# A transformer block on one core: TensorE's pieces at other places in the batch and in the set-up, the other engines' hand-overs reordered

## The chip, the cores and the metric

The kernel runs on one core of one Trainium2 chip. The metric is the time of one launch on the device in microseconds (us). One execution was also profiled; its rows are in a section of their own further down. Engines are named as the profile does: PE (matmuls), PEld (its weight loads), DVE (vector), ACT (scalar), POOL (GpSimd) and SP, which here only issues transfers. A kernel line such as L559 is line 559 of the kernel before; all five engine programs call the same small helper functions, so a line in the profile names a helper, and its place in the program is told by its time.

## The reference

A block with attention and a feed-forward net side by side, for 16 batches of 512 tokens and 256 features:

```
xn = layernorm(x)                                  # 16 x 512 x 256
q, k, v = xn @ wq, xn @ wk, xn @ wv                # 8 heads of 128; q and k rotated (RoPE)
p = softmax(q k' / 128 with a causal mask)         # 512 x 512 for each batch and head
attn = (p @ v) @ wo
h = relu([xn, -xn] @ (+-1 weights k0) * s0) * 2    # 1024 wide
h = relu(h @ (+-1 weights k1) * s1) * 2            # 1024 wide
ffn = h @ (+-1 weights k2) * s2
out = x + attn + ffn
```

## The kernel before, in words

Float32 values are carried as pairs of float16, a high and a low part; a product of two such pairs is three matmuls (high-high, high-low, low-high). The high part is written by ACT (`qk_hi`, `v_hi`, `o_hi`, ...), the low part by DVE, which reads the same PSUM bank again and subtracts the high part (`qk_lo` L559, `v_lo` L564, `o_lo` L569, `p_lo` L584, `h0r_lo_low` L593, `h1_lo`). There are eight PSUM banks, and each PE piece takes a whole one, so a piece can start only when the piece that used its bank before has been read by both engines.

A batch is cut into these PE pieces: `qk` (q or k of one head, 6 matmuls), `v_proj` (6), `scores` (12 matmuls in three fills), `values` (18), `layer0` (4 or 8), `product` (the middle layer of the feed-forward net, which in the loop is done by seven products of half the size in place of eight, 16 matmuls a half), `layer2` (32) and `project` (48). In the set-up batch 0 still takes the middle layer whole (`layer1`, 16 matmuls). `qk(g, w)` has g = 8b + head and w = 0 for q, 1 for k; so `scores(8b+1)` belongs to the second head of batch b.

The way of a head: `qk` on PE; ACT copies the two halves crosswise (`swap`, two instructions), DVE multiplies by the cosines (`straight`), POOL by the sines (`crossed` L351), DVE adds (`rotate` L556), ACT writes the high part and DVE the low part (L559); then `scores`; then row maxima on DVE, exponentials on ACT, both halves of the probabilities, a transposing transfer that SP issues (`turn_p`), and `values`, which reads the transposed tile pt. A next batch's normalised input goes the same way through a transposing transfer (`turn_x`, tile xT).

No scheduler decides the order at run time. Each engine has a program written out line by line with its waits (`sync_program` L742, `gpsimd_program` L888, `scalar_program` L1284, `vector_program` L2189, `tensor_program` L3603). Batches 0 and 1 are written out, `for b in range(2, 15)` holds one batch with pieces of batch b+1 and b-1 woven in, and a tail ends the last. The table `ROTATION` (L726) says which bank stands behind each of the loop's eight bank names in a batch. An engine works its list strictly in order, so a piece that stands ahead of another one on DVE delays it although nothing else ties them together.

The set-up: SP issues the loads. DVE takes the statistics of batch 0, turns the three scale factors (tile s, 1.5 KB) into signs (`scale_signs` L483), normalises (`normalise_first` L498), prepares k0 (`subtract_k0` L502), and takes the largest absolute value of each of wq, wk, wv and wo (`largest` L510). PE turns these maxima (`turn_largest`), DVE makes a power of two from them (`power_of_two` L518), and PE spreads it to all partitions:

```
dve.wait_ge(s_s3, 16)
scale_signs(dve)
dve.wait_ge(s_rstd, 1)
normalise_first(dve, 0)
...
largest(dve, 0)          # wq
largest(dve, 1)          # wk
...                      # eight h0_first_lo
power_of_two(dve, 0)     # released: PE's spread_power(0), which all qk need
```

Of the kernel before, what the change touches and what calls it, by code (L numbers as in the profile page):

```python
# [34 lines left out]
def block_kernel(nc, x, wq, wk, wv, wo, k0, k1, k2, s3, cosT, sinT, out):  # L35
    ctx = ExitStack()
    with ctx:
# [702 lines left out]
        ]  # L740

        def sync_program(sp):  # L742
            load_x_first(sp)
            load_x_rest(sp)
            load_scales(sp)
            load_k(sp, 0)
            load_k(sp, 1)
# [3602 lines left out]
```

## Time and profile before

| | |
|---|---|
| time of a launch, median of 3 | 1775.95 us (1774.67 to 1776.29) |
| the profiled execution, its own time | 1776.42 us |
| its span (first to last instruction) | 1774.5 us |
| PE busy | 1721.9 us (97%) |
| DVE, ACT, POOL busy | 1532.1, 1267.3, 927.4 us |
| granted TensorE clock, mean over the span | 0.996 |

The difference between the profiled time and its span, 1.92 us, is what lies around the program. PE is the engine to watch: what it is not busy is 52.6 us of the span, and the rows further down show where these lie and what PE waited for.

### The profile page before, as it was taken

The page shows a single profiled execution, that of the slowest core. Times are in us where ns is not written, and L with a number is a line of the kernel's source. Part 1 is how long each engine was busy: PE and PEld are TensorE (multiplying, and loading weights), DVE is VectorE, ACT ScalarE, POOL GpSimd, SP SyncE. Part 2 cuts the span into 40 slices and gives each one's busy share as a digit, 9 for nine tenths or more (in the row PEclk, how much of TensorE's full clock was granted, in tenths as well). Part 3 has the DMA queues.
Part 4 walks back from the last instruction along what each step waited for, and adds up shares of the span by engine and source line. Part 5 has one row for each costly group of instructions (what it writes and reads, how often), then busy time and mean ns, then how long its engine had stood idle before and what let it go on. Part 6 is the DMA issues. An engine that isn't in the chain of part 4 may idle for free.

```text
span 1774.5 us, 34051 instructions
## 1 busy us (share of the span) xinstructions
PE 1721.9 (97%) x12720; PEld 1195.5 (67%) x12720; DVE 1532.1 (86%) x3630; ACT 1267.3 (71%) x2717; POOL 927.4 (52%) x952
## 2 busy tenths in 40 slices
PE   6899989999999999999999999999999999999999
PEld 2456757767676676767767677676766767677667
DVE  7899888897988979888897988989889798888975
ACT  6677676776867777677776767768677776777763
POOL 6555545555545645464564555555456454655632
PEclk9999999999999999999999999999999999999999
DMA  4234543344343443344344343433434344343433
GB/s 172 48 48 79 93 68 79 66 78 76 63 92 58 87 70 64 86 67 85 59 79 89 63 81 66 78 72 66 87 65 88 67 65 85 67 87 58 80 70 73
DMA packets 454839, 134.09 MB, mean 76 GB/s; under 512 B 434704, under 2 KB 453648, under 8 KB 454672
## 3 DMA queue, kind: packets, MB, share of 16 engines
q1 hardware_dynamic: 454672, 131.90, 39.4%
q8 instruction: 100, 1.64, 0.4%
q14 instruction: 67, 0.55, 0.1%
HBM read 14.94 MB, written 8.39 MB: 13 GB/s over the span
## 4 chain that ended last, share of the span: by engine, by line
PE 68%; DVE 20%; POOL 3%; DMA 3%; ACT 3%; issue 2%; SPq 1%; DVEq 0%; POOLq 0%
PE bank L238 32%; PE bank L694 17%; PE bank L678 8%; PE bank L661 8%; DVE ph L584 3%; PE bank L705 3%; DVE bank L556 3%; DVE p L574 3%; DVE qk L559 2%; DVE bank L553 2%; DMA pt<-ph 2%; DVE rt L589 1%; POOL xT L342 1%; POOL tb L351 1%; ACT p L426 1%
## 5 line engine op out<-in xcount | busy, mean ns | idle before, releaser
L354 POOL TENSOR_SCALAR ph<-p,ri 128x384 f16<-128x384 f32 (+3 forms) x512 | 313.2, 612 | 455.4 <-DVE rk L581 418.2
L351 POOL TENSOR_TENSOR tb<-tb,sin 128x512 f32<-128x512 f32 x256 | 333.0, 1301 | 242.1 <-ACT tb L410 235.2
L694 PE MATMUL bank<-hb,wa 128*128 128x256 f16 x3360 | 379.9, 273 | 0.2 <-ACT bank L442 0.2
L694 PEld LDWEIGHTS bank<-hb,wa 128*128 128x128 fp8e5 x3360 | 328.0, 98 | 41.7 <-ACT bank L442 0.5
L426 ACT ACTIVATE p<-p,nm,sc 128x512 f32<-128x512 f32 (+3 forms) x512 | 328.5, 645 | 1.6
L584 DVE SCALAR_TENSOR_TENSOR ph<-p,rk,ph 128x512 f16<-128x512 f32 (+3 forms) x512 | 310.2, 613 | 0.7 <-POOL ph L354 0.7
L574 DVE CUSTOM_DVE_ANT_0 p<-bank,mask 128x512 f32<-128x512 f32 (+3 forms) x512 | 228.9, 484 | 48.9 <-PE bank L661 46.8
L661 PE MATMUL bank<-qk 128*128 128x512 f16 (+3 forms) x1536 | 231.6, 301 | 14.7 <-DVE qk L559 13.5
L678 PE MATMUL bank<-pt,v 128*128 128x256 f16 (+1 forms) x2304 | 232.5, 255 | 12.9 <-DMA pt<-ph 11.5
L678 PEld LDWEIGHTS bank<-pt,v 128*128 128x128 f16 x2304 | 202.5, 98 | 39.9 <-DMA pt<-ph 17.5
L661 PEld LDWEIGHTS bank<-qk 128*128 128x128 f16 x1536 | 133.3, 98 | 121.3 <-DVE qk L559 21.6
L413 ACT ACTIVATE qk<-bank 128x512 f16<-128x512 f32 x256 | 151.0, 590 | 82.1 <-DVE bank L556 81.7
L559 DVE TENSOR_TENSOR qk<-bank,qk 128x512 f16<-128x512 f32 x256 | 174.3, 681 | 31.4 <-ACT qk L413 30.3
L556 DVE TENSOR_TENSOR bank<-bank,tb 128x512 f32<-128x512 f32 x256 | 177.3, 693 | 19.2 <-POOL tb L351 14.0
L238 PE MATMUL bank<-xT,wq 128*128 128x512 f16 x768 | 186.6, 379 | 1.6 <-DVE v L564 1.6
L409 ACT ACTIVATE tb<-bank 64x512 f32<-64x512 f32 x256 | 151.9, 593 | 50.9 <-PE bank L238 42.9
L238 PE MATMUL bank<-xT,wk 128*128 128x512 f16 x768 | 186.7, 379 | 1.0 <-DVE wk L533 1.0
L238 PE MATMUL bank<-wv,xT 128*128 128x512 f16 x768 | 183.7, 379 | 2.9 <-DMA xT<-rt 2.9
L553 DVE TENSOR_TENSOR bank<-bank,cos 128x512 f32<-128x512 f32 x256 | 176.7, 690 | 4.5 <-ACT tb L410 4.5
L238 PE MATMUL bank<-wo,o 128*128 128x256 f16 x1536 | 172.9, 273 | 0.0
L358 POOL TENSOR_TENSOR hb<-rt,hb 128x1024 f16<-128x1024 f32 x60 | 132.5, 2208 | 62.1 <-ACT hb L439 60.8
L238 PEld LDWEIGHTS bank<-wo,o 128*128 128x128 f16 x1536 | 150.2, 98 | 20.5
(111 smaller groups left out, 2266.3 us busy)
## 6 DMA issues: line engine op xcount, KB each, us to landing
out<-xnat SPq DMA_DIRECT2D x32, 256.0 KB, 2.4
xnat<-in_x SPq DMA_DIRECT2D x15, 512.0 KB, 3.9
pt<-ph SPq DMA_TRANSPOSE x256, 4.3
o<-in_k SPq DMA_DIRECT2D x1, 1024.0 KB, 7.4
v<-in_wq SPq DMA_DIRECT2D x1, 1024.0 KB, 9.4
v<-in_wk SPq DMA_DIRECT2D x1, 1024.0 KB, 11.1
ph<-in_wv SPq DMA_DIRECT2D x1, 1024.0 KB, 13.5
o<-in_wo SPq DMA_DIRECT2D x1, 1024.0 KB, 10.3
```

Of the source, the lines that this page charges most:

```text
L238: m = pe.matmul(ps[:, cols[0]:cols[1]], l, r, start=start and n == 0, stop=signal is not None and n == last)
L351: pool.tensor_tensor(tb, tb, SIN[:], ALU.mult).then_inc(s_crossed, 1)
L354: pool.tensor_scalar(part(g, i, HI), prob(g, i), RI[:, g % 4, i:i + 1], 4096.0, ALU.mult, ALU.mult).then_inc(s_P_hi, 1)
L426: act.activation(prob(g, i), prob(g, i), ACT.Exp, bias=NM[:, g % 4, i:i + 1], scale=SC[:, 0:1], accum_out=SM[:, g % 4, i:i + 1]).then_inc( ...
L553: dve.tensor_tensor(ps[:, :], ps[:, :], COS[:], ALU.mult).then_inc(s_straight, 1)
L556: dve.tensor_tensor(ps[:, :], ps[:, :], TB[:, (2 * g + w) % TRING, :], ALU.add).then_inc(s_rot, 1)
L559: dve.tensor_tensor(QK[:, g % 2, 2 * w + 1, :], ps[:, :], QK[:, g % 2, 2 * w, :], ALU.subtract).then_inc(s_qk_lo, 1)
L574: dve.tensor_tensor_reduce(out=prob(g, i), in0=ps[:, a:a + w], in1=MASK[:, 512 - w:512], scale=1.0, scalar=-3.0e38, op0=ALU.add, op1=ALU.m ...
L584: dve.scalar_tensor_tensor(part(g, i, LO), prob(g, i), RK[:, g % 4, i:i + 1], part(g, i, HI), ALU.mult, ALU.subtract).then_inc(s_P_lo, 1)
L661: mm = pe.matmul(ps[:, col:col + w], l, m, start=i == tiles[0] and n == 0, stop=end)
L678: mm = pe.matmul(ps[:, 128 * i0:128 * i1], l, m, start=n == 1, stop=n == 18)
L694: mm = pe.matmul(ps[:, 256 * u:256 * u + 256], WA[:, w, k, (2 * j + u) * 128:(2 * j + u) * 128 + 128], HB[:, h, s, k, :], start=first and ...
```

## The change

The helpers are the same, and so are the operations. What differs is the order of the calls in all five programs, the waits that go with it, and the banks. Batches 0 to 3 are written out now, and the loop runs over `range(4, 15)` (`range(4, 14)` on ACT and PE); `ROTATION` has 16 rows and repeats every eight batches where it repeated every six. The core of the diff, SP's loads, one row of the table, DVE's set-up and three places of PE's loop:

```diff
         def sync_program(sp):
+            load_x_rest(sp)
             load_x_first(sp)
-            load_x_rest(sp)
+            load_k(sp, 0)
+            load_w(sp, "k")
+            load_w(sp, "q")
             load_scales(sp)
-            load_k(sp, 0)
             load_k(sp, 1)
-            load_w(sp, "q")
-            load_w(sp, "k")
-            load_cos(sp)
+            load_w(sp, "v")
             load_sin(sp)
-            load_k(sp, 2)
-            load_w(sp, "v")
-            load_x(sp, 1)
             sp.wait_ge(s_k0, 4)
             load_w(sp, "o")
+            load_cos(sp)
+            load_x(sp, 1)
+            load_k(sp, 2)
+            sp.wait_ge(s_xp, 1)
+            turn_x(sp, 1)
             sp.wait_ge(s_P_lo, 4)
             sp.wait_ge(s_pad, 1)
             turn_p(sp, 0)
             sp.wait_ge(s_P_lo, 8)
             sp.wait_ge(s_W2, 1)
             turn_p(sp, 1)
-            sp.wait_ge(s_xp, 1)
-            turn_x(sp, 1)
...
         def vector_program(dve):
...
+            dve.wait_ge(s_w_in["k"], 16)
+            largest(dve, 1)
             dve.wait_ge(s_xT_hi, 1)
             xT_first_lo(dve, 0, BANK[0])
             dve.wait_ge(s_xT_hi, 2)
             xT_first_lo(dve, 1, BANK[1])
-            subtract_k0(dve, 1)
-            subtract_k0(dve, 2)
-            subtract_k0(dve, 3)
             dve.wait_ge(s_w_in["q"], 16)
             largest(dve, 0)
-            dve.wait_ge(s_w_in["k"], 16)
-            largest(dve, 1)
             dve.wait_ge(s_h0_hi, 1)
-            h0_first_lo(dve, 0, BANK[2])
+            h0_first_lo(dve, 3, BANK[2])
+            dve.wait_ge(s_w_in["v"], 16)
+            largest(dve, 2)
...
+            dve.wait_ge(s_w_in["o"], 16)
+            largest(dve, 3)
...
+            dve.wait_ge(s_x[1], 16)
+            stats(dve, 1)
             dve.wait_ge(s_am_max, 1)
             power_of_two(dve, 0)
...
         def tensor_program(pe):
...
+            for b in range(4, 14):
+                ps = [BANK[i] for i in ROTATION[b]]
...
+                qk(pe, 8 * b + 9, 1, ps[4])
+                pe.wait_ge(s_h1, 8 * b)
+                scores(pe, 8 * b + 8, 0, ps[2])
...
+                qk(pe, 8 * b + 10, 1, ps[4])
+                pe.wait_ge(s_vp, 8 * b + 11)
+                v_proj(pe, b + 1, 0, 2, ps[3])
...
+                pe.wait_ge(s_qk_lo, 16 * b + 22)
+                v_proj(pe, b + 1, 1, 3, ps[4])
```

**SP, the first loads.** These are rows of the difference on SP. The names are the tiles and the inputs; o and v and ph are also the places where weights wait until they are split.

```order
+L249 DMA xnat<-in_x 128x2x256
 L245 DMA xnat<-in_x 128x2x256
-L249 DMA xnat<-in_x 128x2x256
+L259 DMA o<-in_k 128x4x256
+L267 DMA v<-in_wk 128x2x1024
+L267 DMA v<-in_wq 128x2x1024
 L255 DMA s<-in_s 128x3
-L259 DMA o<-in_k 128x4x256
 L259 DMA o<-in_k 128x8x256
-L267 DMA v<-in_wq 128x2x1024
-L267 DMA v<-in_wk 128x2x1024
+L267 DMA ph<-in_wv 128x2x1024
```

The scales s stood third, behind the two halves of x; now k0 (0.5 MB), wk and wq (1 MB each) go ahead of them.

**DVE, from the first transposed input to the power of two.** Before (L506 writes xT's low part, L510 is `largest`, L545 the low part of h0, L518 to L524 the power of two):

```order
L506 SCALAR_TENSOR_TENSOR xT<-bank,xT 128x4x128 x2
L502 TENSOR_TENSOR w<-o 128x2x256 x3
L510 TENSOR_REDUCE p<-v 128x1 x2
L545 SCALAR_TENSOR_TENSOR hb<-bank,hb 128x512 x5
L514 TENSOR_REDUCE ar<-bank 128x1
L545 SCALAR_TENSOR_TENSOR hb<-bank,hb 128x512 x3
L518 TENSOR_SCALAR ar<-ar 128x1
L521 TENSOR_SCALAR ar<-ar 128x1
L524 TENSOR_SCALAR dg<-ident,ar 128x2
```

Now:

```order
L510 TENSOR_REDUCE p<-v 128x1
L506 SCALAR_TENSOR_TENSOR xT<-bank,xT 128x4x128 x2
L510 TENSOR_REDUCE p<-v 128x1
L545 SCALAR_TENSOR_TENSOR hb<-bank,hb 128x512
L510 TENSOR_REDUCE p<-ph 128x1
L545 SCALAR_TENSOR_TENSOR hb<-bank,hb 128x512 x4
L510 TENSOR_REDUCE p<-o 128x1
L545 SCALAR_TENSOR_TENSOR hb<-bank,hb 128x512 x3
L514 TENSOR_REDUCE ar<-bank 128x1
L456 BN_STATS bn<-xnat 128x6 x4
L461 BN_AGGR mv<-bn 128x2 x4
L464 TENSOR_SCALAR ve<-mv 128x4
```

One `largest` moved ahead of xT's low part, the two of wv and wo (p<-ph, p<-o) and the statistics of batch 1 (L456 to L464) moved ahead of the power of two, which follows these rows. The three subtractions of L502 moved ahead of the first row.

**PE in the loop, batch 6, between k of its second head and that head's scores.** Before (after the row wk of head 1; with bank numbers, as rows would read alike):

```order
L238 MATMUL bank7<-xT,wk 128x512 x6
L238 MATMUL bank3<-wv,xT 128x512 x6
L661 MATMUL bank6<-qk 128x512 x3
...
L661 MATMUL bank1<-qk 128x256 x3
L678 MATMUL bank4<-pt,v 128x256 x9
...
L238 MATMUL bank0<-xT,wq 128x512 x6
L238 MATMUL bank6<-xT,wk 128x512 x6
L661 MATMUL bank3<-qk 128x512 x3
```

Now, from the same k of head 1 to its scores and on to the v projection that follows (the wk of bank 0 behind the scores is k of head 2, and the last row, on the same bank, is `v_proj(b, 1, 3)`):

```order
L238 MATMUL bank0<-xT,wk 128x512 x6
L661 MATMUL bank7<-qk 128x512 x3
...
L705 MATMUL bank4<-w2,h1 128x256 x32
L238 MATMUL bank5<-wv,xT 128x512 x6
L238 MATMUL bank7<-xT,w0 128x512 x4
L238 MATMUL bank2<-xT,w0 128x512 x4
L678 MATMUL bank6<-pt,v 128x256 x9
...
L661 MATMUL bank1<-qk 128x512 x3
```

```order
L238 MATMUL bank0<-xT,wk 128x512 x6
L238 MATMUL bank5<-wv,xT 128x512 x6
L238 MATMUL bank6<-xT,w0 128x512 x4
L238 MATMUL bank1<-xT,w0 128x512 x4
L238 MATMUL bank3<-xT,wq 128x512 x6
L238 MATMUL bank4<-xT,w0 128x512 x4
L238 MATMUL bank5<-xT,w0 128x512 x4
L238 MATMUL bank0<-wv,xT 128x512 x6
```

Between k of head 1 and its scores there now stands a whole `layer2` (w2,h1, 32 matmuls), and no other `qk`. The last fence is the hand-over of one bank from k of head 2 to a v projection, with five pieces between them.

## Rows read from the trace of the kernel before

**Rows 1.** The page, part 1: busy us (share of the span), instructions.
```profile
PE 1721.9 (97%) x12720; PEld 1195.5 (67%) x12720; DVE 1532.1 (86%) x3630; ACT 1267.3 (71%) x2717; POOL 927.4 (52%) x952
```

**Rows 2.** Stretches: us; busy PE, PEld, DVE, ACT, POOL; PEclk, DMA, GB/s.
```profile
25.98:90.20 64.22, 52.77 (x246) 24.22 (x245) 53.97 (x107) 43.13 (x80) 36.90 (x37) 0.92 0.18 34
90.20:270.00 179.80, 170.47 (x1220) 113.37 (x1219) 160.08 (x388) 133.54 (x296) 93.41 (x100) 0.99 0.44 71
270.00:1700.00 1430.00, 1413.72 (x10616) 996.33 (x10615) 1251.35 (x2980) 1037.27 (x2233) 758.11 (x769) 1.00 0.40 74
372.09:479.61 107.52, 106.45 (x802) 75.06 (x801) 94.24 (x226) 78.34 (x169) 57.12 (x58) 1.00 0.41 75
```

**Rows 3.** Waits of PE over the span: us in total, times, longest.
```profile
PE bank L661 <- DVE qk L559: 13.5, 16, 2.9
PE bank L678 <- DMA pt<-ph: 11.5, 20, 2.2
...
PE bank L238 <- DMA xT<-rt: 2.9, 3, 1.4
```

**Rows 4.** PE in batch 6: start, us, instruction, idle before it.
```profile
674.62 3.66 PE L705 MATMUL bank<-w,h 128*128 128x256 fp8e5 x32
678.94 1.82 PE L678 MATMUL bank<-pt,v 128*128 128x256 f16 x18 [0.66 <-DMA pt<-ph]
...
683.62 1.46 PE L238 MATMUL bank<-xT,wk 128*128 128x512 f16 x6
...
692.93 1.80 PE L661 MATMUL bank<-qk 128*128 128x512 f16 x12 [0.69 <-DVE qk L559]
```

**Rows 5.** Timeline of DVE, just ahead of the wait at 692.
```profile
691.20 0.47 DVE L584 SCALAR_TENSOR_TENSOR ph<-p,rk,ph 128x256 f16<-128x256 f32 x1
691.59 0.68 DVE L564 SCALAR_TENSOR_TENSOR v<-bank,v 128x512 f16<-128x512 f32 x1
692.20 0.67 DVE L559 TENSOR_TENSOR qk<-bank,qk 128x512 f16<-128x512 f32 x1
```

**Rows 6.** The page, part 5: the multiplication on POOL inside the rotation.
```profile
L351 POOL TENSOR_TENSOR tb<-tb,sin 128x512 f32<-128x512 f32 x256 | 333.0, 1301 | 242.1 <-ACT tb L410 235.2
```

**Rows 7.** Timeline of the loads that SP issues at the start.
```profile
1.73 0.46 SPq L255 DMA_DIRECT2D s<-in_s  x1
...
3.26 0.86 SPq L267 DMA_DIRECT2D v<-in_wq  x1
```

**Rows 8.** Loads until 30 us: KB each, us to landing.
```profile
v<-in_wq SPq DMA_DIRECT2D x1, 1024.0 KB, 9.4
...
s<-in_s SPq DMA_DIRECT2D x1, 1.5 KB, 3.2
```

**Rows 9.** Timeline of DVE in the set-up.
```profile
7.54 1.38 DVE L498 TENSOR_SCALAR rt<-xnat,mv,rs 128x256 f32<-128x256 f32 x4 [0.86 <-POOL rs L326]
...
10.71 0.69 DVE L506 SCALAR_TENSOR_TENSOR xT<-bank,xT 128x512 f16<-128x512 f32 x1 [0.50 <-ACT xT L365]
11.80 0.69 DVE L506 SCALAR_TENSOR_TENSOR xT<-bank,xT 128x512 f16<-128x512 f32 x1 [0.41 <-ACT xT L365]
...
14.35 4.47 DVE L510 TENSOR_REDUCE p<-v 128x1 f32<-128x2048 f32 x2
19.10 3.08 DVE L545 SCALAR_TENSOR_TENSOR hb<-bank,hb 128x512 f16<-128x512 f32 x5 [0.29 <-ACT hb L399]
...
59.04 1.40 DVE L456 BATCH_NORM_STATS2 bn<-xnat 128x6 f32<-128x256 f32 x4
```

**Rows 10.** Timeline of PE in the set-up.
```profile
25.98 0.28 PE L238 MATMUL bank<-dg,p 128*128 128x2 f32 x2
26.12 2.75 PE L238 MATMUL bank<-hb 128*128 128x512 f16 x12
...
39.19 5.33 PE L238 MATMUL bank<-hb 128*128 128x512 f16 x12
...
58.15 3.38 PE L661 MATMUL bank<-qk 128*128 128x512 f16 x12 [2.95 <-DVE qk L559]
```

More of the change, by code:

```diff
@@ L2424, in vector_program @@
[L2424 to L2437 removed]
+            qk_lo(dve, 4, 1, BANK[1])
@@ L3916, in tensor_program @@
[L3916 to L3924 removed]
+            product(pe, 1, 6, range(8), BANK[1])
+            pe.wait_ge(s_vp, 14)
+            product(pe, 1, 5, range(8), BANK[3], first=True)
+            pe.wait_ge(s_o, 11)
@@ new lines, in tensor_program @@
+            pe.wait_ge(s_h1, 11)
+            qk(pe, 22, 1, BANK[5])
+            pe.wait_ge(s_o, 17)
+            v_proj(pe, 2, 1, 0, BANK[3])
+            pe.wait_ge(s_pt[1], 288)
+            pe.wait_ge(s_s5, 4)
+            values(pe, 17, BANK[4])
+            pe.wait_ge(s_pt[0], 320)
+            pe.wait_ge(s_qk_lo, 45)
+            values(pe, 18, BANK[2])
+            product(pe, 0, 4, range(8), BANK[1])
+            pe.wait_ge(s_vp, 22)
+            scores(pe, 21, 0, BANK[3])
+            pe.wait_ge(s_o, 18)
@@ new lines, in tensor_program @@
+            scores(pe, 21, 1, BANK[4])
+            pe.wait_ge(s_qk_lo, 46)
+            scores(pe, 21, 2, BANK[5])
+            pe.wait_ge(s_o, 19)
+            qk(pe, 23, 1, BANK[2])
+            product(pe, 1, 2, range(8), BANK[6])
+            pe.wait_ge(s_h1, 12)
+            v_proj(pe, 2, 1, 2, BANK[1])
+            product(pe, 1, 7, range(8), BANK[7])
+            pe.wait_ge(s_pt[1], 320)
+            pe.wait_ge(s_max, 85)
+            values(pe, 19, BANK[3])
+            pe.wait_ge(s_max, 88)
@@ new lines, in tensor_program @@
+            v_proj(pe, 2, 1, 1, BANK[5])
+            pe.wait_ge(s_h1, 13)
+            qk(pe, 23, 0, BANK[6])
+            pe.wait_ge(s_copy, 12)
+            product(pe, 1, 4, range(8), BANK[4])
+            pe.wait_ge(s_qk_lo, 47)
+            scores(pe, 22, 0, BANK[2])
+            pe.wait_ge(s_vp, 23)
+            scores(pe, 22, 1, BANK[1])
+            pe.wait_ge(s_o, 20)
+            scores(pe, 22, 2, BANK[3])
+            pe.wait_ge(s_pt[0], 352)
+            pe.wait_ge(s_vp, 24)
+            values(pe, 20, BANK[7])
@@ new lines, in tensor_program @@
+            pe.wait_ge(s_xT, 48)
+            v_proj(pe, 3, 0, 1, BANK[5])
+            pe.wait_ge(s_qk_lo, 48)
+            scores(pe, 23, 0, BANK[4])
+            scores(pe, 23, 1, BANK[2])
+            scores(pe, 23, 2, BANK[6])
+            pe.wait_ge(s_max, 91)
+            qk(pe, 24, 1, BANK[1])
+            pe.wait_ge(s_max, 92)
+            qk(pe, 24, 0, BANK[3])
+            pe.wait_ge(s_o, 21)
+            layer2(pe, 0, BANK[7])
+            product(pe, 1, 3, range(8), BANK[0])
+            pe.wait_ge(s_max, 93)
@@ new lines, in tensor_program @@
+            layer2(pe, 0, BANK[6])
+            product(pe, 1, 3, range(8), BANK[1])
+            pe.wait_ge(s_max, 125)
+            qk(pe, 34, 0, BANK[0])
+            pe.wait_ge(s_pt[1], 480)
+            pe.wait_ge(s_vp, 33)
+            values(pe, 29, BANK[4])
+            pe.wait_ge(s_max, 127)
+            v_proj(pe, 4, 0, 0, BANK[7])
+            pe.wait_ge(s_max, 128)
+            layer0(pe, 4, 0, 0, BANK[3])
+            layer0(pe, 4, 0, 1, BANK[3])
+            pe.wait_ge(s_ffn, 7)
+            layer0(pe, 4, 4, 0, BANK[6])
@@ new lines, in tensor_program @@
+            pe.wait_ge(s_h1, 107)
+            qk(pe, 118, 1, BANK[2])
+            pe.wait_ge(s_o, 113)
+            v_proj(pe, 14, 1, 0, BANK[1])
+            pe.wait_ge(s_pt[1], 1824)
+            pe.wait_ge(s_s5, 28)
+            values(pe, 113, BANK[7])
+            pe.wait_ge(s_pt[0], 1856)
+            pe.wait_ge(s_qk_lo, 237)
+            values(pe, 114, BANK[5])
+            product(pe, 0, 4, range(8), BANK[3])
+            pe.wait_ge(s_vp, 118)
+            scores(pe, 117, 0, BANK[1])
```

6882 lines of the change are left out of this document (4504 added, 2378 removed), and 25 rows, old and new, of the table ROTATION.

## The prediction

> **What bounds the kernel now.** I read the page first: PE is busy 97% of the span, DVE 86% [rows 1]. PE's work is the same before and after, so the change can only win from the 52.6 us (1774.5 - 1721.9) in which PE is idle, and can lose without a limit. Then the stretches [rows 2]: in the set-up from 25.98 to 90.20 PE is idle 11.45 us (64.22 - 52.77); from 90.20 to 270 it is idle 9.33; from 270 to 1700, thirteen and a third batches (1430 / 107.52), 16.3. The other 15.5 are the time before 25.98, most of it before the first transposed input, and the tail. One batch of the loop is 107.52 us with 106.45 busy, so 1.07 idle. The view of waits says on what [rows 3]: on the low part of q and k (13.5 us, 16 times), on the transposed probabilities (11.5, 20 times), and on the transposed input (2.9, 3 times). In batch 6 the two waits are 0.66 ahead of `values` and 0.69 ahead of the scores of head 1 [rows 4]. The last of these is read on DVE: right ahead of the low part that PE waits for stand a `p_lo` and a `v_lo` that nobody waits for at that moment, from 691.20 to 692.20 [rows 5]. So the loop's waits are matters of order and of how many PE pieces lie between, not of DVE's total.
>
> **The loop.** How long a q or k takes from the end of its `qk` to its low part I take from the same place. The k of head 1 starts at 683.62 and needs about 1.3 us (1.46 less what overlaps the next piece); its low part is ready at 692.20 + 0.67 = 692.87 [rows 4, 5]. That is about 7.95 us, DVE's queue and all. Between them lie now v_proj, scores, values and two qk, about 7.2 us; the difference is the wait of 0.7. By the changed order, between this k and its scores lie three fills of scores, one layer2, one v_proj, two layer0 and one values: 1.6 + 3.5 + 1.3 + 1.7 + 1.6 = 9.7 us (scores 1.80, layer2 3.66 and values 1.82 [rows 4], each less about 0.2 by which it overlaps the next piece; v_proj as the k, layer0 as eight of the k's matmuls). That is 1.75 more than the 7.95, so this wait goes (-0.7 a batch). Counted in the same way, `values` now has at least 27 us of PE work behind its scores where the tightest before had 21 to 23, so the 0.35 a batch that the transposed tile costs on average (1.07 less 0.7) goes too, and with `turn_x` issued earlier on SP the three waits on xT (2.9, of which 1.6 lie in this stretch).
>
> What could be late next are the hand-overs of banks, which are tighter than before. The worst is shown in the last order fence: k of head 2 and `v_proj(b, 1, 3)` share a bank with five pieces, 6.0 us, between them. The price of this wait is bounded from both sides. The bare way has six steps: one on POOL at 1.30 [rows 6] and five at about 0.65 like `qk_lo`'s 0.67 [rows 5], 4.5 us, which fits in 6.0: no wait. With the queue that the 7.95 contains, it would be 1.9 us a batch. DVE's list ahead of this low part is shorter now (it has its own place by urgency), and one such foreign pair was 1.0 us [rows 5]; I take 0.4. All other hand-overs that I followed, `product` and `qk` included, come out within 0.2. That leaves 0.6 idle in a batch where 16.3/13.3 = 1.22 were: 16.3 - 13.3 x 0.6 = 8.3, so -8.3 over 270 to 1700, between -15 (no wait) and +9 (1.9 a batch, 25.3 less 16.3).
>
> **Batches 0 to 2, 90.20 to 270.** These were written out with more idle time, 9.33 [rows 2], in single waits on the transposed tiles and on v's low part. The changed order keeps more PE work behind the scores here too. At its tightest place, the first values of batch 0, I count 16.5 us of PE work for the way of the probabilities, short by about 0.5. I take 2.8 idle, which is the loop's old rate of 1.22 on 1.67 batches and 0.8 for the start: -6.5, between -8.5 and 0.
>
> **The set-up.** Two edits speak against the change here. First the scales: DVE has `scale_signs` ahead of its first `normalise_first`. Before, they were issued third, at 1.73, and landed 3.2 us later [rows 7, 8], long before their use. Now k0, wk and wq are issued ahead. In the trace the loads land in the order of issue, and with the same 3 MB ahead wq landed 9.4 us after 3.26 [rows 7, 8]; so I put the scales at about 12.4 (-0.3 for one transfer that is smaller than wq). Normalising starts at about 12.75 instead of 7.54 [rows 9]: +5.2. The Trainium skill, page "DMA: Bandwidth & Descriptors", section "Queues, rings and completion order", states that a DMA is split over up to 16 rings, which are not ordered among each other, so a small later transfer may be done before larger earlier ones. By that rule the table would come earlier than I say; no row here shows a small load overtaking. What it would do here, worked out: issued at about 4 (1.73 + 0.5 + two issues of 0.86) [rows 7], 3.2 on its way [rows 8], so ready at 7.2, 5.2 earlier; of that about half would reach the spread, 2.7, since DVE then stands before weights that have not landed (wo last of all).
>
> Second, DVE's order: two more `largest` (4.47 for two [rows 9]) and the statistics of batch 1 (1.40 [rows 9] and about 0.5 in small ones) stand ahead of the power of two. Three waits of DVE, 0.50, 0.41 and 0.29 [rows 9], fall away as ACT is ahead by then. So `spread_power(0)`, on which all q and k hang, comes at 25.98 [rows 10] + 5.2 + 4.5 + 1.9 - 1.2 = 36.4, 10.4 later.
>
> For this PE gets a set-up with its inputs ready. From this instruction to the end of batch 0's last `layer1` the pieces are the same ones before and after: seven layer1, eight qk, three scores, four v_proj, one values. Before they took 64.22, of it 52.77 busy [rows 2]. In the busy time are matmuls at a lower granted clock: after two long waits of PE (2.95 us the second) twelve matmuls of layer1 took 5.33 instead of 2.75, and the scores 3.38 instead of 1.80 [rows 4, 10], together 4.2; in this stretch the granted clock is 0.92 [rows 2]. So the pure work is 48.6. The waits that made the 11.45 were, by their releasers in the timeline, for the two later `largest`, for split weights and for low parts such as the 2.95. With all four maxima early I find, by the same counting, what is left: 0.6 at the second power, 1.4 at the third scores, 0.5 at the values; 2.5. PE waits longer ahead of the spread now, so the slow matmuls can come there: 0 to 2.6 (5.33 - 2.75), taken as 0.7, as layer1(0) keeps PE at work shortly before. End: 36.4 + 48.6 + 2.5 + 0.7 = 88.2 against 90.2: -2, between -7 (scales early, no wait) and +3.
>
> **The tail** has the same pieces, and one wait of the longest kind on the transposed tile (2.2 [rows 3]) more or fewer is its price: 0, between -2.2 and +2.2.
>
> **The sum**, against the profiled execution: 1774.5 - 8.3 - 6.5 - 2 = 1757.7 of span, with 1.92 around it 1759.6. The profiled execution (1776.42) was 0.47 above the median of the runs, so 1759.1.
>
> **The rivals.**
> - *All hand-overs hold* (no wait in the loop, scales early as in the case above): -15 in place of -8.3 and -4.7 in place of -2: 1749.7. For it: my way of counting gave 1.1 us for the wait at 692.93, which is 0.69, so it overstates. Against it: the landing order.
> - *The waits only move.* DVE's pieces stay at 86%, and what is put ahead at one place is behind at another: the loop keeps its 1.07, and the start gains half of what I say. -1.6 for xT and -3 for the start: 1771.3. For it: before, it was pieces of the same length that delayed each other; against it: the 9.7 us above.
> - *Slower: the tighter banks decide.* Place: `v_proj(b, 1, 3)` behind k of head 2. If its low part takes the 7.95 us as before, PE waits 1.9; with 0.6 at the pieces behind it on PE, 2.5 a batch in place of 1.22: 33 - 16.3 = +17 over the loop, and with -6 at the start 1774.5 + 17 - 6 + 1.4 = 1787. It decides from an idle time of about 1.9 a batch on, where the loop gives back what the start gains. For it: the hand-over in [rows 4, 5] was measured at 7.95; against it: some of that was foreign pieces on DVE (1.0 right ahead of it), which the change reorders.
> - *Set-up alone is worse* is not a case of its own: at worst +3 against -14.8.
>
> **How the numbers follow.** A difference of 0.2%, 3.55 us, is about what a measurement of this kernel can tell from no change: 1772.4 to 1779.5 is "same". Chances: the forecast 0.60 (1749 to 1769 with the bounds above), all hand-overs hold 0.13, the waits only move 0.14 (a third of it inside the 0.2%), slower 0.13. Faster: 0.60 + 0.13 + 0.09 = 0.82; same 0.05; slower 0.13. The range from 1747 to 1772 leaves out the slower case, a third of the waits that only move and little of the case in which all holds: 2 in 10. The forecast's own range is 1749 to 1769.
>
> **What would show it.** In the profile after: the scales landing near 12.4 and DVE's first normalise behind them; `spread_power(0)` near 36.4 and batch 0's last layer1 ending near 88; no wait of 0.7 for a low part ahead of the scores of head 1; a period of the loop near 107.0 to 107.1; no wait on xT. It would be wrong if the period is above 108 (then look at the v projection behind k of head 2), or if the spread comes later than 40, which would move the whole start.

## The result: 34 us slower, and the profile after

The changed kernel took 1809.44 us (median, 1805.85 to 1811.32) against 1775.31: a ratio of 1.0191, 95% interval 1.0178 to 1.0204. The forecast was 1759 with a range from 1747 to 1772. The profiled execution has a span of 1807.5 us, 33.0 more than before.

The page's part 1, which answers to [rows 1]:

```profile
PE 1722.1 (95%) x12720; PEld 1192.9 (66%) x12720; DVE 1627.5 (90%) x3630; ACT 1271.4 (70%) x2717; POOL 929.0 (51%) x952
```

PE's busy time is what it was (1721.9). DVE's has grown by 95.4 us, from 1532.1, although it runs the same 3630 instructions. Busy time by stretch, with the columns of [rows 2]: the set-up from the first `spread_power` to the start of batch 0's last layer1 tail, the stretch to 270, and one period of the loop.

```profile
36.44:90.56 54.12, 48.29 (x240) 23.15 (x241) 45.78 (x90) 38.55 (x72) 31.89 (x32) 0.97 0.13 25
90.50:270.00 179.50, 172.42 (x1215) 113.95 (x1213) 166.97 (x388) 131.54 (x290) 92.64 (x99) 0.98 0.42 74
567.02:677.17 110.15, 106.67 (x801) 74.88 (x801) 100.66 (x226) 78.38 (x169) 57.04 (x58) 1.00 0.41 73
```

The period is 110.15 us in place of 107.52 (the mean of before over thirteen batches, from the scores of head 1 at 260.71 to those at 1661.84, was 107.78), with 100.66 busy on DVE in place of 94.24. The waits of PE over the span, which answer to [rows 3], and the timeline of PE in one batch, which answers to [rows 4]:

```profile
PE bank L661 <- DVE qk L559: 23.9, 14, 2.3
PE bank L238 <- DVE qk L559: 18.4, 13, 1.5
...
PE bank L678 <- DMA pt<-ph: 9.7, 7, 3.6
```

```profile
667.62 1.46 PE L238 MATMUL bank<-xT,wq 128*128 128x512 f16 x6
...
677.17 1.80 PE L661 MATMUL bank<-qk 128*128 128x512 f16 x12 [1.77 <-DVE qk L559]
...
693.89 1.46 PE L238 MATMUL bank<-xT,wk 128*128 128x512 f16 x6
...
704.98 1.79 PE L661 MATMUL bank<-qk 128*128 128x512 f16 x12
706.61 1.46 PE L238 MATMUL bank<-xT,wk 128*128 128x512 f16 x6
...
715.56 1.47 PE L238 MATMUL bank<-wv,xT 128*128 128x512 f16 x6 [1.45 <-DVE qk L559]
```

Two new waits stand in each batch of the loop: 1.77 us ahead of the scores of head 7, for the low part of its q (the `wq` row at 667.62 is its `qk`), and 1.45 ahead of `v_proj(b, 1, 3)`, for the low part of k of head 2 (the `wk` row at 706.61). The wait of before, at the scores of head 1 (704.98), is gone, and so are the waits on the transposed input. Now DVE and POOL around these waits, which answer to [rows 5] and [rows 6]:

```profile
669.95 0.80 DVE L584 SCALAR_TENSOR_TENSOR ph<-p,rk,ph 128x512 f16<-128x512 f32 x1
...
671.27 2.09 DVE L584 SCALAR_TENSOR_TENSOR ph<-p,rk,ph 128x384 f16<-128x384 f32 x2
673.29 0.69 DVE L553 TENSOR_TENSOR bank<-bank,cos 128x512 f32<-128x512 f32 x1
...
676.43 0.68 DVE L559 TENSOR_TENSOR qk<-bank,qk 128x512 f16<-128x512 f32 x1
...
690.35 1.26 DVE L581 TENSOR_SCALAR rk<-ri 128x4 f32<-128x4 f32 x1
...
703.64 0.68 DVE L559 TENSOR_TENSOR qk<-bank,qk 128x512 f16<-128x512 f32 x1
...
708.78 2.75 DVE L584 SCALAR_TENSOR_TENSOR ph<-p,rk,ph 128x512 f16<-128x512 f32 x3
711.45 0.69 DVE L553 TENSOR_TENSOR bank<-bank,cos 128x512 f32<-128x512 f32 x1
...
714.83 0.67 DVE L559 TENSOR_TENSOR qk<-bank,qk 128x512 f16<-128x512 f32 x1
```

```profile
668.85 2.71 POOL L354 TENSOR_SCALAR ph<-p,ri 128x512 f16<-128x512 f32 x4 [6.21 <-DVE rk L581]
671.63 1.45 POOL L351 TENSOR_TENSOR tb<-tb,sin 128x512 f32<-128x512 f32 x1
...
690.32 1.26 POOL L351 TENSOR_TENSOR tb<-tb,sin 128x512 f32<-128x512 f32 x1 [3.34 <-ACT tb L410]
...
709.38 1.33 POOL L351 TENSOR_TENSOR tb<-tb,sin 128x512 f32<-128x512 f32 x1 [0.33 <-ACT tb L410]
```

Read the two together. At 671.27 two p_lo take 2.09 us, while POOL multiplies by the sines from 671.63 to 673.08; DVE's next instruction, the `straight` of the q that PE needs, starts at 673.29. At 708.78 three p_lo take 2.75 us, beside POOL's multiplication from 709.38 to 710.71; the `straight` of k starts at 711.45, and its low part (714.83) ends at 715.50, where PE goes on. At 690.35 an instruction over 128x4 elements (L581) takes 1.26 us and ends as POOL's, begun at 690.32, ends. Beside POOL's short instructions for the high parts (`p_hi`, L354, at 668.85) little is lost: the p_lo of 512 columns at 669.95 takes 0.80, and one at 693.91 takes 0.74. The groups of DVE by shape (count, busy us, mean ns), before and after:

```profile
L584 DVE SCALAR_TENSOR_TENSOR ph<-p,rk,ph 128x512 f16<-128x512 f32 x128 | 108.7, 849 | 0.0
...
L584 DVE SCALAR_TENSOR_TENSOR ph<-p,rk,ph 128x384 f16<-128x384 f32 x128 | 81.9, 640 | 0.4 <-POOL ph L354 0.4
...
L581 DVE TENSOR_SCALAR rk<-ri 128x4 f32<-128x4 f32 x128 | 21.9, 171 | 4.4
```

```profile
L584 DVE SCALAR_TENSOR_TENSOR ph<-p,rk,ph 128x512 f16<-128x512 f32 x128 | 138.7, 1084 | 3.8 <-POOL ph L354 2.7
L584 DVE SCALAR_TENSOR_TENSOR ph<-p,rk,ph 128x384 f16<-128x384 f32 x128 | 120.0, 937 | 1.9 <-POOL ph L354 1.9
...
L581 DVE TENSOR_SCALAR rk<-ri 128x4 f32<-128x4 f32 x128 | 41.9, 327 | 4.4
```

All 512 p_lo together went from 310.2 to 397.7 us of busy time (613 to 796 ns in the mean), L581 from 21.9 to 41.9: 107.5 us more, which is DVE's growth and a little over. The multiplications by the sines are not alone in this. Counted instruction by instruction against what the same shapes take with POOL idle, p_lo and L581 were 37 us over before and are 151 over now: beside the multiplications 9 and 88, beside POOL's two other long kinds (`h0t_lo` L358 and `xp_lo` L347, 2.1 to 2.2 us each) 15 and 51. At 612.94 one p_lo of 512 columns takes 2.50 us, while L358 runs from 612.77 to 614.90.

The Trainium skill, page "SBUF — State Buffer", section "SBUF: two separate sides", says that DVE and GpSimd share one pair of SBUF ports as an exclusive lock for a whole instruction, and that a DVE instruction with two SBUF inputs needs it against a GpSimd instruction that reads SBUF. The rows agree: p_lo reads two tiles in SBUF and is long beside POOL's work, while `straight`, `rotate` and `qk_lo`, which read PSUM, keep 0.69, 0.68 and 0.67. L581 reads one tile and so is no case of that sentence; that it waits too, the row at 690.35 shows.

The set-up after, PE and DVE, which answers to [rows 9, 10]:

```profile
36.44 0.38 PE L238 MATMUL bank<-dg,p 128*128 128x2 f32 x2 [1.78 <-DVE dg L524]
36.68 4.44 PE L238 MATMUL bank<-hb 128*128 128x512 f16 x12
...
55.91 0.38 PE L238 MATMUL bank<-dg,p 128*128 128x2 f32 x2 [1.62 <-DVE dg L524]
...
77.33 1.80 PE L661 MATMUL bank<-qk 128*128 128x512 f16 x12 [1.78 <-DVE qk L559]
...
86.31 1.82 PE L678 MATMUL bank<-pt,v 128*128 128x256 f16 x18 [2.43 <-DMA pt<-ph]
...
90.56 1.03 PE L238 MATMUL bank<-hb,rt 128*128 128x512 f16 x4
```

```profile
13.44 0.17 DVE L483 TENSOR_SCALAR sg<-s 128x3 f32<-128x3 f32 x1 [7.24 <-DMA s<-in_s]
...
13.72 1.05 DVE L498 TENSOR_SCALAR rt<-xnat,mv,rs 128x256 f32<-128x256 f32 x3
```

### The profile page after: what moved, and what is told of

Read it like the earlier page. It is cut to its first block, busy times and chain, and to the rows that moved or that the text cites. A ratio compares the mean times of both kernels' runs of the same rounds, so it can differ in the third digit from the quotient of the medians.

```text
span 1807.5 us, 34023 instructions
## 1 busy us (share of the span) xinstructions
PE 1722.1 (95%) x12720; PEld 1192.9 (66%) x12720; DVE 1627.5 (90%) x3630; ACT 1271.4 (70%) x2717; POOL 929.0 (51%) x952
## 4 chain that ended last, share of the span: by engine, by line
DVE 42%; PE 21%; ACT 15%; issue 10%; POOL 9%; DMA 2%; SPq 1%; DVEq 0%; POOLq 0%
DVE ph L584 12%; PE bank L238 10%; ACT p L426 6%; DVE p L574 5%; POOL tb L351 4%; DVE bank L556 4%; DVE bank L553 4%; DVE qk L559 4%; PE bank L694 3%; DVE rt L589 3%; PE bank L705 3%; PE bank L678 3%; POOL xT L342 3%; PE bank L661 2%; POOL ph L354 2%
## 5 line engine op out<-in xcount | busy, mean ns | idle before, releaser
L354 POOL TENSOR_SCALAR ph<-p,ri 128x512 f16<-128x512 f32 (+3 forms) x512 | 312.2, 610 | 500.0 <-DVE rk L581 460.3
L351 POOL TENSOR_TENSOR tb<-tb,sin 128x512 f32<-128x512 f32 x256 | 339.7, 1336 | 226.4 <-ACT tb L410 220.0
L584 DVE SCALAR_TENSOR_TENSOR ph<-p,rk,ph 128x512 f16<-128x512 f32 (+3 forms) x512 | 397.7, 796 | 6.2 <-POOL ph L354 5.0
L694 PE MATMUL bank<-hb,wa 128*128 128x256 f16 x3360 | 391.2, 273 | 1.6 <-DVE qk L559 1.6
L661 PE MATMUL bank<-qk 128*128 128x512 f16 (+3 forms) x1536 | 234.3, 301 | 27.9 <-DVE qk L559 23.9
L409 ACT ACTIVATE tb<-bank 64x512 f32<-64x512 f32 x256 | 151.9, 593 | 109.7 <-PE bank L238 102.3
L574 DVE CUSTOM_DVE_ANT_0 p<-bank,mask 128x512 f32<-128x512 f32 (+3 forms) x512 | 224.2, 480 | 3.0 <-PE bank L661 2.9
L410 ACT ACTIVATE tb<-bank 64x512 f32<-64x512 f32 x256 | 150.6, 588 | 3.1
```

Source lines behind the costliest of these rows:

```text
L351: pool.tensor_tensor(tb, tb, SIN[:], ALU.mult).then_inc(s_crossed, 1)
L354: pool.tensor_scalar(part(g, i, HI), prob(g, i), RI[:, g % 4, i:i + 1], 4096.0, ALU.mult, ALU.mult).then_inc(s_P_hi, 1)
L574: dve.tensor_tensor_reduce(out=prob(g, i), in0=ps[:, a:a + w], in1=MASK[:, 512 - w:512], scale=1.0, scalar=-3.0e38, op0=ALU.add, op1=ALU.m ...
L584: dve.scalar_tensor_tensor(part(g, i, LO), prob(g, i), RK[:, g % 4, i:i + 1], part(g, i, HI), ALU.mult, ALU.subtract).then_inc(s_P_lo, 1)
L661: mm = pe.matmul(ps[:, col:col + w], l, m, start=i == tiles[0] and n == 0, stop=end)
L694: mm = pe.matmul(ps[:, 256 * u:256 * u + 256], WA[:, w, k, (2 * j + u) * 128:(2 * j + u) * 128 + 128], HB[:, h, s, k, :], start=first and ...
```

## The experiments

Theory A, formed on these rows: two hand-overs have too little PE work over them (6.3 us for q of head 7, 6.0 for k of head 2), because p_lo stand ahead of them on DVE and are stretched by POOL. Its rival, theory B: DVE's load as a whole is the bound, and PE's waits are only where it comes out. Each run has the kernel before beside it on the same chip; its median was 1773.7 to 1775.7, so differences of a few us between runs of different chips are read from the ratios.

**DVE's order at both places (e1).** Three p_lo go behind the low part of q of head 7, which also moves ahead of a row maximum. Of the three p_lo ahead of the `straight` of k of head 2 the first stays, the second goes behind the steps up to `rotate`, the third behind the low part, which moves ahead of three `difference` too:

```diff
                 v_lo(dve, 1, 1, ps[4])
-                dve.wait_ge(s_P_hi, 32 * b - 10)
-                p_lo(dve, 8 * b - 3, 2)
-                dve.wait_ge(s_P_hi, 32 * b - 9)
-                p_lo(dve, 8 * b - 3, 1)
                 dve.wait_ge(s_swap, 16 * b)
                 straight(dve, ps[3])
-                dve.wait_ge(s_P_hi, 32 * b - 8)
-                p_lo(dve, 8 * b - 3, 0)
...
+                qk_lo(dve, 8 * b - 1, 0, ps[3])
...
-                qk_lo(dve, 8 * b - 1, 0, ps[3])
...
+                p_lo(dve, 8 * b - 3, 2)
...
-                p_lo(dve, 8 * b, 2)
...
-                p_lo(dve, 8 * b, 1)
...
                 straight(dve, ps[5])
...
+                p_lo(dve, 8 * b, 2)
...
+                qk_lo(dve, 8 * b + 2, 1, ps[5])
...
+                p_lo(dve, 8 * b, 1)
...
-                qk_lo(dve, 8 * b + 2, 1, ps[5])
```

> The changed kernel, DVE's loop alone edited at two places: the low parts of the probabilities (p_lo L584) that stand ahead of the hand-over of q of head 7 (two of them) and of k of head 2 (three of them) are put behind it. Theory A (two hand-overs of q or k are too short of PE work, 6.3 and 6.0 us, because p_lo pieces stand ahead of them on DVE and POOL's multiplication by the sines stretches those): the waits of 1.77 and 1.45 us a batch fall below 0.4 each, the period from 110.17 to 107.2 to 107.8, the time to 1777 to 1784 us. Theory B (DVE, busy 90% in the span and with 95 us more than before, is the bound, and PE's waits are only where this comes out): the same DVE work is there, the waits come back elsewhere, the period stays above 109.3 and the time above 1800.

Measured: 1793.31 us (ratio to before 1.0108, 1.0091 to 1.0125), 16 less than the change by the medians and 15 by the ratios, between the two theories. The timeline of PE over one period and its start:

```profile
590.68 1.80 PE L661 MATMUL bank<-qk 128*128 128x512 f16 x12 [0.66 <-DVE qk L559]
...
601.39 1.80 PE L678 MATMUL bank<-pt,v 128*128 128x256 f16 x18 [0.28 <-DVE hb L597]
...
605.72 3.12 PE L238 MATMUL bank<-wo,o 128*128 128x256 f16 x27 [0.23 <-DVE o L569]
...
631.05 1.92 PE L694 MATMUL bank<-hb,wa 128*128 128x256 f16 x16 [0.25 <-DVE qk L559]
...
634.05 1.19 PE L661 MATMUL bank<-qk 128*128 128x384 f16 x9 [0.38 <-DVE mx L574]
```

Both waits are gone, as A said, and the period is 108.91. But five others stand there: 0.66 at the scores of head 1, 0.28, 0.23, 0.25 and 0.38.

**One of the two at a time (e9, e10).**

> The changed kernel with only the first of the two edits of DVE's order (three p_lo behind the low part of q of head 7; the other hand-over as it was). If the two waits are independent, the one of 1.77 us goes and the other stays at 1.45: 11 x 1.5 to 1.77 = 16 to 19 us less, 1790 to 1794. If DVE's queue is so full that a wait mended here opens the next, the gain is under 10 us, above 1799, and other waits grow in the timeline.

> The changed kernel with only the second edit (two p_lo and three small pieces behind the low part of k of head 2, for whose bank the v projection waits). Independent: the wait of 1.45 goes, 11 x 1.45 = 16 us less, 1791 to 1796. Full queue: under 8 us less, above 1801; with both edits 16 us came out in place of 35.

Measured: 1806.67 (1.0181, 1.0162 to 1.0200) and 1803.46 (1.0162, 1.0143 to 1.0180), so 3 and 6 us less by the medians (2 and 5 by the ratios), not 16 each; the first can't be told from no gain, as its interval overlaps that of the change. With only the first mended, the other wait grew from 1.45 to 1.75 and 0.66 opened at the scores of head 1; with only the second, the first stayed at 1.77, and 0.23 and 0.25 opened elsewhere. One row of PE's timeline from each:

```profile
602.98 1.47 PE L238 MATMUL bank<-wv,xT 128*128 128x512 f16 x6 [1.75 <-DVE qk L559]
```

```profile
566.51 1.80 PE L661 MATMUL bank<-qk 128*128 128x512 f16 x12 [1.77 <-DVE qk L559]
```

A mended wait opens the next: the part of A by which the two waits are the whole loss falls, and B gains.

**More PE work over the two hand-overs (e2).**

```diff
+                product(pe, 1, 3, range(8), ps[2])
                 pe.wait_ge(s_qk_lo, 16 * b + 16)
                 scores(pe, 8 * b + 7, 0, ps[1])
...
                 layer2(pe, 0, ps[3])
-                product(pe, 1, 3, range(8), ps[2])
...
-                pe.wait_ge(s_qk_lo, 16 * b + 22)
-                v_proj(pe, b + 1, 1, 3, ps[4])
...
                 values(pe, 8 * b + 7, ps[7])
+                pe.wait_ge(s_qk_lo, 16 * b + 22)
+                v_proj(pe, b + 1, 1, 3, ps[4])
```

(ACT's copy of this v projection waits for it, as it now ends later.)

> The changed kernel, PE's loop alone edited at the same two places: one product (1.75 us) moves ahead of the scores that wait for q of head 7, and one values (1.65 us) ahead of the v projection that waits for k of head 2's bank; DVE's order stays. Theory A: the covers grow from 6.3 to 8.0 and from 6.0 to 7.7 us, so the waits fall from 1.77 and 1.45 to about 0 to 0.2, the period to 107.0 to 107.6, the time to 1776 to 1783. Theory B: DVE gets no faster by this, the waits move on, the time stays above 1800.

Measured: 1820.74 us (1.0258, 1.0243 to 1.0273), 11 more than the change. The timeline of PE:

```profile
591.81 1.80 PE L661 MATMUL bank<-qk 128*128 128x512 f16 x12 [0.67 <-DVE qk L559]
...
603.42 1.80 PE L678 MATMUL bank<-pt,v 128*128 128x256 f16 x18 [2.17 <-DVE hb L597]
```

Neither old wait is left, but `values`, moved ahead, now waits 2.17 us for the low part of h0 that frees its bank and stands right behind the same `qk_lo` on DVE. The edit moved one piece and shortened another hand-over by as much; it speaks for B, but it was not a clean test.

One reading over these runs says more than any single wait. In the change, e1, e2, e9 and e10 DVE is busy 100.66, 98.97, 100.99, 99.81 and 100.03 us in a period, and the periods are 110.15, 108.91, 110.47, 109.74 and 109.78: each time 9.5 to 9.9 more. What an edit of the order gave went with what it took off DVE's work, whichever waits of PE it moved.

**POOL's share (e4, e7).** POOL multiplies 128 columns instead of 512, in the changed kernel and in the one before:

```diff
-            pool.tensor_tensor(tb, tb, SIN[:], ALU.mult).then_inc(s_crossed, 1)
+            pool.tensor_tensor(tb[:, 0:128], tb[:, 0:128], SIN[:, 0:128], ALU.mult).then_inc(s_crossed, 1)
```

> The changed kernel, in which POOL multiplies only 128 of the 512 columns by the sines (and ACT's crosswise copy carries a factor of 1/16, so that the numbers stay small): part of the rotation is left out. Theory A with the stretch as its cause: p_lo on DVE, 796 ns in the mean, falls to 540 to 620, DVE's busy time by 70 to 100 us, both waits vanish, the period is 106.7 to 107.3 and the time 1772 to 1780. If p_lo is long for another reason (its own waits for the high parts on POOL, or queueing), its mean stays above 750 ns and DVE's busy time within 30 us of 1627.

> The kernel before with the same cut as the changed kernel had in the run with the short sine (128 of 512 columns on POOL, part of the rotation left out). If the sine's instruction costs the changed kernel more by what it does to DVE than by its own length, the kernel before, whose p_lo are stretched little (613 ns in the mean), gains only its loop's waits, 8 to 16 us, to 1758 to 1766, against the 57 us that the changed kernel gained; then the changed order with this cut (1752.7) is faster than the old order with it. If the cut shortens every hand-over alike and that is all, both gain alike, 40 us or more.

Measured: 1752.68 us for the changed kernel (0.9875, 0.9861 to 0.9890), 57 less; 1777.70 for the one before (1.0015, 1.0006 to 1.0024), 2.5 more. The page of the first, and one period of its loop:

```profile
PE 1713.7 (98%) x12720; PEld 1196.3 (68%) x12720; DVE 1560.1 (89%) x3630; ACT 1273.0 (73%) x2717; POOL 706.3 (40%) x952
```

```profile
553.95:660.05 106.10, 106.10 (x801) 75.22 (x800) 95.98 (x225) 78.22 (x170) 42.42 (x59) 1.00 0.45 75
```

DVE's busy time fell by 67 us, the mean of p_lo from 796 to 676 ns (less than theory A expected of both), and in the loop PE waits for nothing: 106.10 busy of 106.10. The time is below A's range. The kernel before got nothing from an instruction that is 0.8 us shorter in each hand-over (1301 to 496 ns); its p_lo went from 613 to 628 ns, as they met POOL's work at other places (beside L358 they are 30 us over where they were 14). Neither expectation for it came true. In the order of before, then, a shorter way alone gives nothing. For the changed order these two runs can't tell the shorter way from what DVE no longer loses beside POOL; the next run is for that. And with the same cut in both, the changed order is 25 us faster than the old one.

**DVE's load with POOL's work untouched (e5).**

```diff
-            dve.scalar_tensor_tensor(part(g, i, LO), prob(g, i), RK[:, g % 4, i:i + 1], part(g, i, HI),
+            dve.scalar_tensor_tensor(part(g, i, LO)[:, 0:128], prob(g, i)[:, 0:128], RK[:, g % 4, i:i + 1], part(g, i, HI)[:, 0:128],
```

> The changed kernel, in which DVE writes only 128 columns of each p_lo (the rest of the low part of the probabilities is left out and stands at zero; POOL clears the whole tile once in the set-up). The sine multiplication on POOL, and so the bare way of a q or k, stays as it is. Theory A (DVE's queue, in which p_lo and its stretching stand ahead of the hand-overs, makes them 8 to 10 us long): DVE's busy time falls by 120 to 220 us, the waits of 1.77 and 1.45 us vanish, the time is 1752 to 1775. Rival C (the fixed steps of the way are too long for covers of 6 us, the 1.3 us on POOL above all): the waits stay above 1 us each and the time above 1795.

Measured: 1749.51 us (0.9857, 0.9844 to 0.9870), 60 less and a little below theory A's range. Its page:

```profile
PE 1714.8 (98%) x12720; PEld 1198.6 (68%) x12720; DVE 1513.3 (86%) x3630; ACT 1273.3 (73%) x2717; POOL 886.1 (51%) x946
```

DVE has 114 us less (120 to 220 were expected); no wait is left in the loop, with the same covers of 6.0 and 6.3 us and the sine at its full length. Rival C falls.

**The same load put on the kernel before (e12).**

```diff
+            if i == 3:
+                dve.scalar_tensor_tensor(SPARE[:, g % 2, :], MASK[:], 1.0, MASK[:], ALU.mult, ALU.subtract)
```

> The kernel before with one more DVE instruction for each head, which writes a tile that nobody reads (512 columns, about 0.74 us, right behind the first p_lo): DVE's work in a batch rises from 94.3 to about 100.3 us, what the changed kernel has; PE's order and all hand-overs stay as before. If DVE's load is what makes the waits, whatever PE's order, the time comes near the changed kernel's: 1795 to 1815 us. If the old order's longer covers carry the load and the changed order's short ones (6.0 and 6.3 us) are what counts, the time rises by 3 to 12, to 1778 to 1787.

Measured: 1833.86 us (1.0322, 1.0304 to 1.0339), 59 more and above both forecasts. Its page, and its waits of PE (its helpers' lines are one to three higher, so L560 is `qk_lo`, L664 `scores`, L681 `values`):

```profile
PE 1732.5 (94%) x12720; PEld 1194.9 (65%) x12720; DVE 1632.4 (89%) x3758; ACT 1271.4 (69%) x2717; POOL 982.0 (54%) x952
```

```profile
PE bank L664 <- DVE qk L560: 30.8, 16, 3.7
PE bank L681 <- DMA pt<-ph: 16.2, 14, 3.1
PE bank L681 <- DVE hb L600: 12.8, 10, 1.4
```

With 100 us more on DVE, as the change has, the old order loses still more, so its longer covers don't carry this load. That speaks for B, but the load is not the same in kind: the added instruction reads SBUF itself, POOL's busy time rose by 55 us (`p_hi` took 709 ns in the mean where it took 612), and it stands in the way of the probabilities. Nor does B hold as a matter of DVE's busy share: with the short sine (e4) DVE is busy 90.5% of a period (95.98 of 106.10) and PE waits for nothing, in the change 91.4% (100.66 of 110.15) and PE is idle for 3.48.

**The sine in two halves (e6).** Two instructions of 256 columns; DVE is released behind the second.

> The changed kernel with POOL's multiplication by the sines in two instructions of 256 columns each, the second of which releases DVE. All is computed. If p_lo is long because it waits out a running POOL instruction, it now waits for a half at most: its mean falls from 796 to 640 to 740 ns, DVE's busy time by 30 to 80 us, and the time by 5 to 25, to 1784 to 1804. Rival: the halves together take longer than one (about 1.5 to 1.6 us against 1.34), each rotation comes that much later, p_lo is stretched by the same in sum, and the time is 1809 to 1825.

Measured: 1805.29 us (1.0175, 1.0160 to 1.0189), 4 less by the medians and 3 by the ratios to before, under the 5 that were expected at least, though the rival had it slower still. The mean of p_lo fell to 754 ns and of L581 from 327 to 263, DVE's busy time by 23 us, and the two waits to 1.37 and 1.33, although the two halves take about 1.5 us together and one took 1.34. The mean and DVE's gain, too, are smaller than expected.

**The scales third (e3).**

```diff
             load_x_first(sp)
+            load_scales(sp)
             load_k(sp, 0)
...
             load_w(sp, "q")
-            load_scales(sp)
```

> The changed kernel with the scales' load put back to the third place, behind the two halves of x. Theory A (the prediction's term): the scales land near 5 instead of near 12, DVE normalises from 7.5, the first spread of a power comes 2.7 to 5.2 us earlier than 36.4, and the time falls by 2.5 to 5.5 us, since the loop's loss is untouched: 1804 to 1807. Rival: the largest values of the weights wait for their own loads, so that nothing or under 1.5 us comes out, 1808 to 1810.

Measured: 1805.44 us (1.0175, 1.0160 to 1.0191), 4.0 less by the medians and 2.8 by the ratios, near what the runs can tell, as the intervals overlap. The trace is clearer. Two rows of its PE timeline, the spread and the first values:

```profile
32.44 0.38 PE L238 MATMUL bank<-dg,p 128*128 128x2 f32 x2 [1.96 <-DVE dg L524]
...
82.30 1.82 PE L678 MATMUL bank<-pt,v 128*128 128x256 f16 x18 [2.41 <-DMA pt<-ph]
```

Both come 4.0 us earlier than in the changed kernel (36.44 and 86.31).

**All of it (e11):** e1's two edits, the scales third, the sine in halves.

> The changed kernel with all that helped it so far: both edits of DVE's order, the scales' load third, the sine in two halves. By adding what they gave alone (16, 4 and 3 to 4 us) 1784 to 1788, still above the kernel before; if the halves matter more once the order is mended (they shorten what is left of the stretch), 1776 to 1784; a time below 1774 would show that the changed order can beat the old one with these edits.

Measured: 1797.72 us (1.0128, 1.0110 to 1.0146), 4 more than e1 alone by the medians, with overlapping intervals. The gains don't add. PE's busy time is 1733.0 us here, against 1722.1 in the change, and the waits that the timeline lists in a period (0.62, 0.36, 0.23, 0.31, 0.38) don't make up the period of 109.76; successive pieces show waits of 0.1 to 0.25 us inside them that the list leaves out. Why the halves, which took a little off the change, give nothing here stays open.

**A version that beats both (e8).** In the kernel before, one p_lo goes behind the low part of k of head 1, at the place of [rows 5]:

```diff
-                p_lo(dve, 8 * b - 1, 1)
                 v_lo(dve, 0, 2, ps[1])
                 dve.wait_ge(s_qk_hi, 16 * b + 4)
                 qk_lo(dve, 8 * b + 1, 1, ps[0])
+                p_lo(dve, 8 * b - 1, 1)
```

> The kernel before with one p_lo in DVE's loop moved behind the low part of k of head 1, for which PE waits 0.69 us a batch (the v_lo beside it frees the bank of these scores, so it stays). The reading of the rows ahead of the prediction: p_lo stands in the way with 0.39 us, so the wait falls to 0.3 and the time by 13 x 0.39 = 5 us, to 1768 to 1770. Rival: the 0.39 comes back at the next wait (the transposed probabilities, 0.66 a batch), and the time stays within 1.5 us of before.

Measured: 1772.35 us (0.9982, 0.9974 to 0.9991), 2.9 less than before. The timeline of PE:

```profile
692.04 1.80 PE L661 MATMUL bank<-qk 128*128 128x512 f16 x12 [0.30 <-DVE qk L559]
...
699.32 1.82 PE L678 MATMUL bank<-pt,v 128*128 128x256 f16 x18 [0.26 <-DMA pt<-ph]
```

The wait fell from 0.69 to 0.30, as expected. The gain lies between the two expectations: from 270 to 1700 PE is idle 12.4 us where it was 16.3, so 3.9 of the 5 came. A small part came back as waits on the transposed probabilities, in single batches (0.26 at 699.32), 12.6 us in all where they were 11.5.

## Why the prediction was wrong

The step that failed is the sentence that left DVE's total aside, "the loop's waits are matters of order and of how many PE pieces lie between, not of DVE's total", and with it the price put on the hand-overs of banks, "I take 0.4", with "All other hand-overs that I followed ... come out within 0.2". Both took DVE's durations from the rows of before, as if the order could not change them. It did: DVE's work in a batch rose from 94.24 to 100.66 us as p_lo and L581 met POOL's long instructions.

- *The way of a q or k.* I set it at 7.95 with the queue and 4.5 without. Counted in the same way it is now 9.1 us for k of head 1 (695.19 to 704.32), 8.2 for q of head 7 (668.92 to 677.11), 7.6 for k of head 2 (707.90 to 715.50). For head 1 the 9.7 of cover was enough, as forecast; for the other two, 6.3 and 6.0 were not (the 6.0 is right, though the fence has six rows between the two ends and not five pieces). How much of this is the stretch can be estimated: in the same batch p_lo of 512, 384 and 256 columns take 0.74, 0.61 and 0.48 where POOL has no long instruction (693.91, 701.45, 703.24), so that the 2.09 and 2.75 us ahead of these two would be about 1.0 and 1.7. By this estimate 1.1 of each wait is the stretch, and 0.7 and 0.4 would be left. The 0.4 is the price that I took for k of head 2; q of head 7 would have missed my 0.2 all the same.
- *The rival that came true* is the third, at the place it named and with nearly its price there: 1.45 of the 1.9 us. It put 2.5 us of idle time on a batch; PE was idle 3.48 (110.15 - 106.67), because q of head 7, which I had passed as within 0.2, cost 1.77. "Some of that was foreign pieces on DVE ..., which the change reorders" was the wrong argument against it: the change put other pieces there, and these are longer. Its time, 1787, was still 22 us too low. (The count against the wait at 692.93 stands there twice with different results: 7.95 less 7.2 is 0.75, while the first rival has 1.1.)
- *The loop:* forecast -8.3. PE's idle time from 270 to 1700 went from 16.3 to 44.2 us, +27.9; in the whole span it grew by 32.8. *The tail*, behind 1700: 7.75 idle where it was 5.2, with 0 forecast.
- *Batches 0 to 2:* idle 7.1 us of 90.5 to 270 where 9.3 were; forecast 2.8. One wait on the transposed probabilities alone is 3.6 us, and one on the low part of q or k 2.3.
- *The set-up:* `spread_power(0)` came at 36.44; forecast 36.4. The scales' wait ended at 13.44, forecast 12.4: issued at 3.3, they were 10.1 us on their way behind larger loads, so the small load did not overtake, as the rows of before had shown. The Trainium skill's page "DMA: Bandwidth & Descriptors" (section "Queues, rings and completion order") leaves open that it does; here it did not. e3 gives the price of this edit: 4.0 us at the spread, where the sum had 5.2. That the sum was met is in part luck: DVE began to normalise at 13.72, 1.0 later than forecast, and from there to the spread it took 4.3 us longer than before, where 5.2 were forecast. After the spread PE was idle 5.8 us, not 2.5 (1.62 at the second power, 1.78 at the third scores, 2.43 at the first values; forecast 0.6, 1.4 and 0.5). Behind the wait of 1.78 at 36.44, the twelve matmuls of layer1 took 4.44 in place of 2.75, 1.7 more where 0.7 was taken; the granted clock from 36.44 to 41.00 is 0.63, most of it at the lower level of 1.2 GHz. Layer1 ended at 91.42 where 88.2 was forecast and 90.20 stood: +1.2 for -2.
- *xT:* no wait on it is left, as forecast.

What is shown: DVE's instructions beside POOL's are what is longer (the rows at 671.27, 690.35 and 708.78, the groups by shape); with less work in DVE's queue and the same covers PE's waits in the loop are gone (e5); and single waits were moved, not taken away, by order alone (e1, e9, e10). Without the loss the changed order would be the faster one: 1752.68 against 1777.70 with the short sine in both (e4, e7). What stays open: how much of the 33 us would go if only the stretching went, as no run takes it away by itself (e4 shortens the way as well, e5 takes work off DVE; the 1.1 us at each hand-over is an estimate); and why the old order loses more from 100 us on DVE than the new one, in part perhaps because POOL was slowed too.

## What to carry to other kernels

Before pricing a reordering by counting the pieces between two ends, check the load of the engine that hands over, in the stretch itself, and take its durations as a result of the order, not as given: look in the trace for instructions of one shape with different durations, and for what ran beside them. A busy share alone doesn't tell whether an engine has room: DVE at 90.5% of a batch made PE wait for nothing (e4), at 91.4% for 3.5 us (the change), and 100 us more on it cost the old order 59. What counts is what stands ahead of each hand-over. A wait mended alone says little; look at what the next hand-over in the queue gains or loses.

## What the runs showed of the hardware that was not expected

p_lo, which reads two SBUF tiles, and one DVE instruction over 128x4 elements wait out a long POOL instruction that began before them: 1.26 us instead of 0.17 for the small one, 2.50 instead of 0.74 for a p_lo of 512 columns, while `straight`, `rotate` and `qk_lo`, which read PSUM, kept their time in the loop. It holds the other way round as well: the four p_hi at 668.85, in the middle of which a p_lo starts, take 2.71 us, and the four at 691.70, beside which none runs until their last, take 2.40. The same instructions in another order so made DVE's busy time 95 us longer. And a load of 1.5 KB took 2.8 us from issue to landing at the third place and 10.1 at the sixth, behind 2.5 MB of weights.
